# Weighing the values in attention: one key tile at a time, or two key tiles in a row with four exp buffers

## The reference

```python
    def _L0_attn_ref(x, W_qkv, W_o):
        ...
        scale = 1.0 / np.sqrt(dk).astype(np.float32)
        attn = jnp.einsum('bhqd,bhkd->bhqk', q, k) * scale
        causal = jnp.tril(jnp.ones((L, L), dtype=bool))
        attn = jnp.where(causal, attn, -jnp.inf)
        attn = jax.nn.softmax(attn, axis=-1)
        y = jnp.einsum('bhqk,bhkd->bhqd', attn, v)
        y = y.transpose(0, 2, 1, 3).reshape(B, L, D)
        return y @ W_o.T
```

## Time and profile before

| | us |
|---|---|
| median of three runs | 2401.53 |
| lowest, highest | 2399.11, 2403.15 |
| the profiled execution: its own time | 2399.69 |
| its span | 2397.8 |
| attention phase within it (first to last instruction) | about 547 to 1061 |

### The profile page before, as it was taken

The page is one execution under the profiler, slowest core; times in us unless marked ns, Lnnn a source line. Parts: engine busy times, 40 slices in busy tenths (PEclk is TensorE's granted clock), DMA queues, the critical chain, the costliest instruction groups (busy, mean ns, idle before and its releaser), DMA issues. The chain is left out here.

```text
span 2397.8 us, 43209 instructions
## 1 busy us (share of the span) xinstructions
PE 2047.2 (85%) x13577; PEld 1400.5 (58%) x13577; DVE 1446.0 (60%) x3844; ACT 996.3 (42%) x2303; POOL 970.0 (40%) x1249
## 2 busy tenths in 40 slices
PE   4359998696999999988289995899988999789996
PEld 3259897352444444437189994566665666456674
DVE  4313223667888888826623333889857676488883
ACT  1023332241666666653133332333325666534332
POOL 4422223750111111124612224666546666455652
PEclk9999999796999999999589997999999999999999
DMA  5145554346333344210255553000000000000002
GB/s 189 39 158 195 192 193 136 118 146 97 54 55 54 54 54 54 28 38 1 70 188 192 195 192 125 22 13 18 0 1 2 2 2 2 1 1 0 0 0 70
DMA packets 105499, 177.02 MB, mean 74 GB/s; under 512 B 14576, under 2 KB 70160, under 8 KB 105360
## 3 DMA queue, kind: packets, MB, share of 16 engines
q1 hardware_dynamic: 99216, 158.47, 24.0%
q0 software_dynamic: 6144, 16.79, 2.2%
HBM read 136.01 MB, written 38.93 MB: 73 GB/s over the span
## 5 line engine op out<-in xcount | busy, mean ns | idle before, releaser
L1024 DVE TENSOR_REDUCE a_part_max<-a_psS 128x1 f32<-128x512 f32 (+3 forms) x608 | 362.8, 655 | 76.2 <-PE a_psS L952 67.6
L1080 ACT ACTIVATE a_PT<-a_psE 128x512 f32<-128x512 f32 (+1 forms) x608 | 309.3, 583 | 189.1 <-PE a_psE L966 174.1
L518 PE MATMUL e_psH<-e_xsT,e_w 128*128 128x128 f32 x2240 | 266.7, 278 | 0.0
L518 PEld LDWEIGHTS e_psH<-e_xsT,e_w 128*128 128x128 f32 x2240 | 259.9, 194 | 0.6
L946 PE MATMUL a_psS<-a_sk,a_sq 96*128 96x512 bf16 (+3 forms) x768 | 234.3, 341 | 23.5 <-DMA a_sk<-qk_parts 19.6
L527 PE MATMUL e_psY<-wo_moe,e_gT 128*128 128x256 f32 x1120 | 253.0, 379 | 0.0
L927 POOL TENSOR_SCALAR_AFFINE_SELECT a_PT<-a_PT 128x512 f32<-128x512 f32 x128 | 81.5, 637 | 419.1 <-ACT a_PT L1080 419.1
L966 PE MATMUL a_psE<-a_sq,a_sk 98*128 98x512 bf16 (+3 forms) x768 | 224.6, 329 | 2.5 <-ACT a_PT L1080 1.4
L527 PEld LDWEIGHTS e_psY<-wo_moe,e_gT 128*128 128x128 f32 x1120 | 207.6, 190 | 25.4
L547 ACT ACTIVATE e_gT<-e_psH,e_bias 128x128 f32<-128x128 f32 x560 | 159.9, 369 | 138.6 <-PE e_psH L518 138.6
L567 DVE TENSOR_TENSOR e_y<-e_psY,e_xr 128x256 f32<-128x256 f32 x70 | 29.7, 425 | 308.1 <-PE e_psY L527 303.9
(11 more groups left out here) (269 smaller groups left out, 3869.1 us busy)
## 6 DMA issues: line engine op xcount, KB each, us to landing
e_w<-w_in SPq DMA_DIRECT2D x70, 1024.0 KB, 4.9
a_sq<-qk_parts SPq DMA_DIRECT2D x96, 128.0 KB, 4.4
a_sk<-qk_parts SPq DMA_DIRECT2D x96, 128.0 KB, 7.2
e_xs<-sorted_x SPq DMA_DIRECT2D x70, 128.0 KB, 2.1
e_xr<-sorted_x SPq DMA_DIRECT2D x70, 128.0 KB, 4.6
sorted_y<-e_yo SPq DMA_DIRECT2D x70, 128.0 KB
sorted_x<-zeros SPq DMA_DIRECT2D x1, 4480.0 KB, 18.8
X<-x_in SPq DMA_DIRECT2D x4, 1024.0 KB, 9.7
```

What stands on the lines that cost most here:

```text
L518: mm = pe.matmul(psH[p][:, n * P:(n + 1) * P], w1[p][:, k, n * P:(n + 1) * P], xsT[p][:, k, :], start=k == 0, stop=k == KD - 1)
L1024: dve.tensor_reduce(part_max[:, c, h0:h0 + heads, qt], psS[place % RING][:, 0:heads * n].rearrange("p (h k) -> p h k", h=heads), AX.X, ALU ...
L1080: act.activation(PT[kt % 2][:, h0:h0 + heads, q0:q0 + n], psE[e % RING][:, 0:heads * n].rearrange("p (h q) -> p h q", h=heads), ACT.Exp, s ...
```

## The change

Key tiles are weighed in pairs: behind slot 18 both 0 and 1, behind 29 both 2 and 3, behind 37 both 4 and 5, and behind slot 2 of the next round both 6 and 7. `PT` has four buffers, of 1024, 896, 768 and 640 columns a head; buffer `kt % 4` starts at query tile `kt % 4`, since a key tile has no queries before itself. The wait of the exps on the weighing goes back four key tiles in place of two. The instructions themselves are the same ones in the same number.

```diff
@@ -797,6 +797,7 @@
     RING = 3
     LEAD = 9
     LAG = 3
+    PTS = 4
     HALF = BT // 2
 
     s_pieces = []
@@ -833,7 +834,7 @@
                 yield "s", u // S, u % S
             if j == turn_slot and it + 1 < ITS:
                 yield "max", it + 1, 0
-            for kt in range(BT):
+            for kt in range(1, BT, 2):
                 due = last_e[kt] + LAG
                 if due < E and j == due and it < ITS:
                     yield "weigh", it, kt
@@ -865,13 +866,18 @@
         neg_max = sb("neg_max", [P, HG, BT])
         max_bf = sb("max_bf", [P, 4, HG * BT], BF16)
         maxT = [sb(f"maxT{i}", [2 * HG * BT, P], BF16) for i in (0, 1)]
-        PT = [sb(f"PT{i}", [P, HG, SEQ]) for i in (0, 1)]
+        PT = [sb(f"PT{i}", [P, HG, SEQ - i * P]) for i in range(PTS)]
         ou = sb("ou", [P, SEQ])
         inverse = [sb(f"inverse{i}", [P, HALF, HG]) for i in (0, 1)]
         psS = [ps(f"psS{i}", [P, 512]) for i in range(RING)]
         psE = [ps(f"psE{i}", [P, 512]) for i in range(RING)]
         psO = ps("psO", [P, SEQ])
         block = ctx.enter_context(nc.Block())
+
+        def exps_of(kt, heads, q0, q1):
+
+            first = kt % PTS * P
+            return PT[kt % PTS][:, heads, q0 - first:q1 - first]
 
         def values(it):
             b, g = it // GROUPS, it % GROUPS
@@ -923,7 +929,7 @@
                     if kt == HALF and it + 1 < ITS:
                         set_v(it + 1)
                     pool.wait_ge(e_drained, it * E + last_diagonal[kt] + 1)
-                    hidden = PT[kt % 2][:, :, kt * P:(kt + 1) * P]
+                    hidden = exps_of(kt, slice(0, HG), kt * P, (kt + 1) * P)
                     pool.affine_select(out=hidden, in_=hidden, compare_op=ALU.is_ge, fill=0.0, base=0,
                                        pattern=[[0, HG], [1, P]], channel_multiplier=-1).then_inc(cleared, 1)
 
@@ -969,20 +975,22 @@
                                    start=i == 0, stop=True, skip_group_check=True)
                 mm.then_inc(e_filled, 1)
 
-            def weigh(it, kt):
-                pe.wait_ge(e_drained, it * E + last_e[kt] + 1)
-                pe.wait_ge(cleared, it * BT + kt + 1)
-                if kt == 0:
+            def weigh(it, last):
+
+                pe.wait_ge(e_drained, it * E + last_e[last] + 1)
+                pe.wait_ge(cleared, it * BT + last + 1)
+                if last == 1:
                     pe.wait_ge(v_set, 4 + it + 1)
                     if it > 0:
                         pe.wait_ge(o_out, o_place["out", it - 1, 1] + 1)
-                for c in range(kt // HALF, 2):
-                    q0 = max(kt * P, c * 512)
-                    for h in range(HG):
-                        mm = pe.matmul(psO[32 * h:32 * h + 32, q0:(c + 1) * 512], va[it % 2][:, kt, h, :],
-                                       PT[kt % 2][:, h, q0:(c + 1) * 512], start=kt == 0,
-                                       stop=kt == HALF * (c + 1) - 1, skip_group_check=True)
-                mm.then_inc(weighted, 1)
+                for kt in (last - 1, last):
+                    for c in range(kt // HALF, 2):
+                        q0 = max(kt * P, c * 512)
+                        for h in range(HG):
+                            mm = pe.matmul(psO[32 * h:32 * h + 32, q0:(c + 1) * 512], va[it % 2][:, kt, h, :],
+                                           exps_of(kt, h, q0, (c + 1) * 512), start=kt == 0,
+                                           stop=kt == HALF * (c + 1) - 1, skip_group_check=True)
+                    mm.then_inc(weighted, 1)
 
             def turn_max(it):
                 out = free_s(s_place["max", it, 0])
@@ -1073,11 +1081,11 @@
                 e = it * E + j
                 act.wait_ge(e_filled, e + 1)
                 q0 = (c + 1) * 512 - n
-                if kt >= 2:
-                    act.wait_ge(weighted, it * BT + kt - 1)
+                if kt >= PTS:
+                    act.wait_ge(weighted, it * BT + kt - PTS + 1)
                 elif it > 0:
-                    act.wait_ge(weighted, (it - 1) * BT + (HALF if c == 0 else BT) - 1 + kt)
-                act.activation(PT[kt % 2][:, h0:h0 + heads, q0:q0 + n],
+                    act.wait_ge(weighted, (it - 1) * BT + kt + 1 + (PTS if c else 0))
+                act.activation(exps_of(kt, slice(h0, h0 + heads), q0, q0 + n),
                                psE[e % RING][:, 0:heads * n].rearrange("p (h q) -> p h q", h=heads), ACT.Exp,
                                scale=float(HD) ** -0.5).then_inc(e_drained, 1)
 
```

## The result

| | before | after |
|---|---|---|
| median, us | 2400.34 (6 runs) | 2408.21 (6 runs) |
| lowest, highest | 2398.60, 2403.64 | 2401.46, 2411.81 |
| ratio, 95% interval | 1 | 1.0029, 1.0019 to 1.0040 |
| profiled execution, own time | 2399.69 | 2407.19 |
| its span | 2397.8 | 2405.3 |

The change makes the kernel slower by 0.29%, 7 us (4.6 to 9.6). The forecast was +2.2 us, with the range 2396 to 2413 around it.

A forecast was written before the change was run, and what follows sets the result against it. VectorE's pace after bursts, not TensorE alone, was taken to bound the kernel. Round 0 +0.6, rounds 1 to 13 +2.6, start of round 14 about 0, end -1.0: +2.2 us, median 2403.7, range 2396 to 2413.

The forecast's parts named there:

- What bounds the kernel: Attention rounds: TensorE looks busy for 29.47 of 29.66 us, but VectorE sets the pace once the ring refills after bursts.
- new waiting: Steady attention round: 1.16 us of added waiting for VectorE against 0.96 us freed on TensorE.
- The price of a burst: Weighing bursts on TensorE: 0.146 us + 1.674 ns a column to the next exp piece; 0.24 us a burst is no streaming.
- The stretches: Four parts of a steady round, forecast to change by +0.49, +0.22, -0.28 and -0.23 us, together +0.20 us.
- Slots 19 to 29: Stretch ending with the joined burst of key tiles 2 and 3: 0.22 us longer, run at VectorE's pace.
- the other handoffs: From the end of a VectorE reduction to the TensorE piece needing its bank: 0.055 us, as for s27 behind reduction 24.
- The last round: End of attention, paced by ScalarE: the change wins 1.0 us from slot 19 of round 14 to the end.
- the signs by which it was to be recognised: Steady round 29.8 to 29.9 us, four bursts, VectorE dry some 2.8 and 1.3 us, s27 0.06 us behind reduction 24.
- The likeliest case: Whole kernel: change within the 0.2% (4.8 us) that cannot be told from none, 2399 to 2408 us; chance 0.60.
- rival 2: Joined burst of key tiles 0 and 1 finds one piece fewer in VectorE's ring: +11.2 us, 2412.7; chance 0.14.
- Rival 1: TensorE's saving comes through whole: 0.96 us a round over 15.5 rounds, 14.9 us, giving 2386.6; chance 0.13.
- Rival 3: Pairs do not run as one piece because GpSimd's clearing comes last: +9.4 us, 2410.9; chance 0.03.

The follow-up runs named there:

- half reductions: Kernels before and after the change, with every maximum reduction reading only the left half of its piece; 2369.96 and 2360.90 us.
- singles4: Kernel before with the four exp buffers alone, each key tile weighed singly at its old place; 2402.02 us, ratio 1.0004.
- after_half_reduce: Changed kernel with every maximum reduction reading only the left half of its piece; 2360.90 us, ratio 0.9827 to the kernel before.
- halves_short: Kernel before with four buffers, key tiles 0 and 1 each weighed in two halves, 4+5 and 6+7 joined; 2389.45 us, ratio 0.9947.
- short_pairs: Kernel before with four buffers, only key tiles 4+5 and 6+7 joined, 0 to 3 weighed singly; 2395.92 us, ratio 0.9971.
- halves_short_ring42: Key tiles 0 and 1 in halves, 4+5 and 6+7 joined, plus four PSUM banks for maximum pieces and two for exp pieces; 2411.87 us, ratio 1.0054 to before.
- after_ring42: Changed kernel with four PSUM banks for maximum pieces and two for exp pieces, instead of three each; 2416.65 us, ratio 1.0063 to the kernel before.

## Why the prediction was right, and where it was not

- **What bounds the kernel.** Right: TensorE's 99% is not a bound of its own. The half reductions show VectorE's share: 1.33 us of the round before are waits for it, and 2.61 of the round after. The forecast had 1.16 us of new waiting; it is 1.28.
- **The price of a burst.** Right to 0.01 us: 3.36, 2.50, 1.64 and 0.79 us to the next exp piece for 1920, 1408, 896 and 384 columns, where 0.146 us + 1.674 ns a column gives 3.36, 2.50, 1.65 and 0.79. That joining saves 0.24 us each was confirmed with VectorE's pace out of the way (0.96 us for four).
- **The stretches.** Slots 3 to 18: 12.86 (12.89 forecast); 30 to 37: 6.36 (6.30); 0 to 2: 2.32 (2.33). Slots 19 to 29: 8.44, forecast 8.34. This is the term that was most mis-sized in the steady round: I let piece 0 of the next round follow the end of reduction 35 by the 0.055 us of the other handoffs. Reduction 35 ended at 730.97 (two pitches of 0.466 and five of 0.60 behind 726.35, and 0.685), and piece 0 came at 731.11, 0.14 later and 5.41 us behind e19, where I had 5.31. The trace of the kernel before has this longer handoff once, ahead of round 0, where VectorE sets the pace: reduction 35 ends at 582.23, and piece 0 of round 1 comes 0.15 us later.

```profile
582.38 0.58 PE L946 MATMUL a_psS<-a_sk,a_sq 96*128 96x128 bf16 x4
```

  Piece 15, which covers four heads as well, follows its reduction there by 0.058 us. So the number of heads is not the reason. Piece 0 is the one piece that also waits for the loads of its round (L948 after, L942 before); whether that wait is the 0.09 us, no run separates. The round is +0.32 in place of +0.20, 1.8 us over 15 rounds.
- **The last round.** Forecast 1.0 us won from slot 19 of round 14 to the end; measured 0.8 us lost. singles4 shows that the gain of the buffers is there (0.7 us in the last round), but 1.2 us went to the burst of 2 and 3 at the low clock. The other 0.6 us are spread over slots 19 to 37 of round 14 and the last round. That the clock could fall in a round in which TensorE waits for ScalarE was not among the steps.
- **The sum.** The attention length of the two traces, split as the prediction split it:

  | part of the phase | forecast, us | measured, us |
  |---|---|---|
  | round 0 | +0.6 | +0.60 |
  | rounds 1 to 13 | +2.6 | +4.15 |
  | round 14, slots 0 to 18 | about 0 | +0.24 |
  | from slot 19 of round 14 to the end | -1.0 | +0.82 |
  | together | +2.2 | +5.8 |

  The time moved by 7 us (4.6 to 9.6). The direction, the mechanism and the signs by which it was to be recognised were right, except that the round is 29.98 us and not 29.8 to 29.9. The likeliest case ("same", 0.60) was not: the measured change lies beyond 0.2%, and the median of 2408.21 lies at the upper end of its 2399 to 2408. The range up to 2413 was drawn for rival 2, which did not happen; it holds the result with room to spare for a reason that was not the forecast's own. Rival 1 (all of 0.96 us) comes true once VectorE is faster. Rival 2 (one piece fewer at slot 18) did not: s27 stands 0.06 us behind reduction 24, and VectorE is dry for 2.87 us, not 3.4. Rival 3 did not: the four joinings of a steady round each keep their 0.24 us in after_half_reduce. At the very end of the phase the last burst does wait for GpSimd, 0.40 us (the row at 1063.83).
- **The rules.** The Trainium skill's rule that changing the tiling mode drains TensorE (TensorEngine Tiling (Array Packing), Key Properties) would have made every switch saved a gain. after_half_reduce agrees that a switch costs TensorE time, 0.24 us; that this is the drain, no run separates. The kernel after shows that the saving need not reach the time.

## What to carry to other kernels

Joining bursts on a busy engine pays only as long as its consumers do not run dry for longer than they can catch up. A first guess for the limit is what they can have queued, here 3 pieces of 0.60 us: the joined bursts of 0.79 and 1.64 us kept their saving, those of 2.50 and 3.36 lost more than they saved, and nothing between was run. It is no sharp limit, for VectorE already ran dry behind single bursts of 1.86 and 1.65 us, and cutting those in halves paid in spite of two more switches. halves_short cuts the long bursts and joins the short ones and is 0.53% faster than the kernel before, where joining everything is 0.29% slower. To find out whether a freed 0.96 us is real, make the other engine's work artificially small in both kernels and compare them stretch by stretch.

## What the runs showed of the hardware that was not expected

- The moment at which TensorE's clock rises again after the barrier behind attention differs between the profiled executions. In the second stretch of 10 us behind the last weighing the granted clock was 0.81 in short_pairs (first fence) and 1.00 before (second fence):

```profile
1061.30:1071.30 10.00, 9.27 (x44) 7.17 (x44) 6.26 (x32) 2.58 (x7) 3.40 (x7) 0.81 0.11 43
```

```profile
1069.40:1079.40 10.00, 9.27 (x55) 7.52 (x56) 7.40 (x35) 3.35 (x9) 4.80 (x10) 1.00 0.12 46
```

  The phases behind attention, which are the same code, took 1338.3 us in the profiled execution before, 1339.0 after, 1343.5 in short_pairs and 1342.9 in halves_short (span less the end of the last weighing). Over all thirteen kernels they took 1335.3 (halves_short_ring42) to 1344.1 us (after_ring42). Whether the kernel or the single execution decides this, one profile of each cannot tell. So a single profiled execution can hide or feign up to 9 us in phases that are not changed; that is why the variants are compared above by round and attention length, and by medians of several runs (whose single runs lie up to 12 us apart).
- A burst of 1408 columns in column groups took 3.73 us to the next exp piece in the last round of the kernel after, where the granted clock over those 3.73 us was 0.66, and 2.50 at a granted clock of 1.00.
